# The opening and the end of a two-layer attention kernel: work moved between steps, the last batch in pairs of tiles, and products of zeros on TensorE

## Chip, cores and metric

One NeuronCore of a Trainium2 chip runs the whole program. The metric is the time of one execution on the device in microseconds: the median of the runs of the kernel before is 555.02 us (three runs, 554.78 to 560.3). A profiled execution of the same kernel took 555.56 us; the span that its trace covers is 553.7 us. "us" in all that follows is a time from the start of that span.

## What is computed

Four sequences (B = 4) of 512 tokens with 256 channels pass through two attention layers of 16 heads with 16 channels each. All inputs and outputs are 32-bit floats.

```
# layer 0
xn = x * rsqrt(mean(x*x) + 1e-6) * rms_w
scale, shift = split(cond @ w_cond)              # cond: (4, 512)
xm = xn * (1 + scale) + shift
q, k, v = split(xm @ w_qkv);  q, k = rope(q), rope(k)
x = softmax(q k^T / 4) v @ w_out + x
# layer 1
xn = layernorm(x, norm_w, norm_b)
q, k, v = xn @ q_w + q_b, xn @ k_w + k_b, (xn @ v_w + v_b) * mask
y = softmax(q k^T + (1 - mask) * -1e6) v
scale, shift = split(silu(cond) @ emb_w + emb_b)
h = layernorm(y, sb_norm_w, sb_norm_b) * (1 + scale) + shift
return x + silu(h) @ out_w + out_b
```

## The kernel before

**Tiles and groups.** Tokens lie in tiles of 128 partitions, `TPB` = 4 tiles a batch. The work on attention is cut into `GROUPS` = 32 groups: 2 layers x 4 batches x 4 groups of heads (`NG`), four heads in each. Group s is step s of one long loop, and a step has four parts, one for each tile k of 128 keys. For a head and a key tile, TensorE makes the scores of 128 keys against 512 queries (`score`, L393), adds the negative row maximum as a second product into the same PSUM bank (`shift`, L404), ScalarE takes the exponential (L561), and TensorE multiplies the probabilities by the values (`values`, L430) into one bank `ACC`. The row maxima come two steps earlier from products with queries and keys exchanged (`row_score`, L413), of which VectorE takes the maximum (L698 in layer 0, L695 in layer 1). Queries and keys are stored as two 16-bit parts each (q_parts, k_parts in device memory) and loaded back in another layout (q_s, k_s).

**Order.** Nothing is planned at run time: the order is written out by hand in tables, and each engine's function walks through the same loop `steps()` and picks its own instructions. `KEY_TILE` (L44) is the order inside one part of a step. `PIECES` (L83) says which other pieces come in which step and part: `turn` (transposes of normalised tokens, L465, with ScalarE's copy to xT, L586 or L599), `qk` (a projection of 128 query or key rows, L476), `v` (value projection, L487), `y` (output projection, L504), `modulate` and `embed` (two products with the condition vector, 32 small products each, L512). p0, f0, p1, f1 name the four places where tokens are turned: before the projections of layer 0, behind its attention, and the same for layer 1. `ROW_SCORES` says which row scores a part makes; steps 0 to 2 hold more than the others. Steps -3 to -1 are the opening, step 32 is the end. The same walk fixes the order of two rings of PSUM banks (`places`, L157): four banks for scores, turns and projections (ScalarE reads them), three for row scores, outputs, y, modulate and embed (VectorE reads them). A piece waits until the bank of its place is read. `turn_shift` (L438) turns the negated maxima, ScalarE copies them (L574) and SyncE moves them into the operand `shift` (L1091).

**Queues.** SyncE issues the loads of x, the tables and the later weights (L1100 to L1117), then `first_parts` (L1051 on) with the part stores of batch 0 (L1039), and the operand loads (L1074). VectorE's `opening` (L751 on) holds the statistics of x (L780 to L788), the normal tiles of batch 0 (L669), the modulation (L812) and the rotation of queries and keys of batch 0 (L798 to L805). ScalarE makes the high part of each (L664). POOL makes the powers (L966, L888), the normal tiles of the later batches, and the rotation of batches 1 to 3 (L912 to L920).

**End.** After the last values product ScalarE copies `ACC` (L568), TensorE turns it (L445), VectorE divides by the sums (L720, L722) and takes the statistics of all 256 channels (L728, L733), POOL makes the power (L886, L888), VectorE the normal tiles (L670), TensorE turns them (L465), ScalarE makes a linear and a tanh image (L599, L600), VectorE multiplies them (L849), TensorE makes the 16 output products (L504), VectorE adds the residual (L744), SyncE stores.

The parts of the two tables that matter:

```
-3: ((("modulate",),) + turn("p0", 0), qk(0, 0, 0, 1, 2, 3), v(0, 0)[:1] + turn("p0", 1) + v(0, 0)[1:],
     qk(0, 1, 0, 1, 2, 3) + v(0, 1)),
-2: (turn("p0", 2), qk(0, 2, 0), qk(0, 2, 1), qk(0, 2, 2)),
-1: (qk(0, 2, 3), (), (("embed",),), ()),
0: ((), (), *one(v(0, 2))),
```

## Time and profile before

| what | value |
|---|---|
| median of the runs | 555.02 us |
| the profiled execution | 555.56 us |
| its span | 553.7 us |
| mean granted TensorE clock over the span | 0.978 |
| busy in the span: TensorE | 516.7 us (93%) |
| VectorE | 408.5 us (74%) |
| ScalarE | 351.6 us (63%) |
| POOL | 213.1 us (38%) |
| moved by DMA | 45.23 MB, mean 82 GB/s |

Busy time is the time in which an engine has an instruction in flight; the products on TensorE are pipelined, so that their busy time says how long the engine has work and not how hard it works. The granted clock is given as a share of 2.4 GHz; 0.5 is 1.2 GHz. PEld is TensorE's weight load, which runs beside the products. A line of the timeline merges neighbouring instructions of the same kind: start, the time that the group takes together, engine, line, operation, output<-inputs, shape, count, and in brackets the idle time of the engine before it with what ended it.

### The profile page before, as it was taken

Reading aid. Unit: us, or ns where it says so; the run is one execution under the profiler, and the core shown is the slowest. Engines: PE = TensorE matmul, PEld = TensorE weight load, DVE = VectorE, ACT = ScalarE, POOL = GpSimd, SP = SyncE. Lnnn points to the kernel's source line nnn. Section 1 sums busy time; section 2 is a strip of 40 time slices with the busy share of each in tenths; the row PEclk is TensorE's granted clock in tenths of the full one; section 3 lists DMA queues with packets and bytes.
Section 4 is the critical chain, followed back from the end, with each engine's and each line's share of the span. In section 5 each row is a group of like instructions: output and inputs, shape, how many; then the busy total and the mean of one; then the engine's idle time right before and its main releaser. Section 6 shows DMA issues by size and latency. Waiting matters only on the chain. (4 is left out here: it accounts for less than half of the span.)

```text
span 553.7 us, 9732 instructions
## 1 busy us (share of the span) xinstructions
PE 516.7 (93%) x3296; PEld 197.1 (36%) x3296; DVE 408.5 (74%) x1056; ACT 351.6 (63%) x682; POOL 213.1 (38%) x223
## 2 busy tenths in 40 slices
PE   5788999999999999999999999999999999999945
PEld 5354432223333344234333344334234232423314
DVE  3586678778888667965898677966988998896032
ACT  1352346667757676776757675766786779678822
POOL 3139999249032350624242340624640034042200
PEclk9999898999999999999999999999999999999986
DMA  7963203143133133110421133111331211120001
GB/s 243 356 200 95 78 3 114 38 118 116 42 112 116 40 109 116 45 40 9 133 91 40 38 115 116 40 38 42 108 118 42 78 41 40 39 78 2 21 19 38
DMA packets 43016, 45.23 MB, mean 82 GB/s; under 512 B 4420, under 2 KB 41556, under 8 KB 42584
## 3 DMA queue, kind: packets, MB, share of 16 engines
q1 hardware_dynamic: 42680, 42.79, 24.7%
q10 hardware_dynamic: 288, 1.84, 0.9%
q8 instruction: 26, 0.43, 0.3%
q14 instruction: 22, 0.18, 0.1%
HBM read 25.46 MB, written 18.87 MB: 80 GB/s over the span
## 5 line engine op out<-in xcount | busy, mean ns | idle before, releaser
L561 ACT ACTIVATE probs<-bank 128x512 f32<-128x512 f32 x512 | 274.2, 597 | 102.7 <-PE bank L404 101.9
L413 PE MATMUL bank<-k_s,q_s 64*128 64x512 f16 x512 | 190.2, 388 | 8.8 <-DVE row_max L695 3.5
L698 DVE TENSOR_REDUCE row_max<-bank 128x1 f32<-128x512 f32 x256 | 162.1, 684 | 38.5 <-PE bank L413 37.0
L695 DVE CUSTOM_DVE_ANT_0 masked<-bank,mask_bias 128x512 bf16<-128x512 f32 x256 | 162.9, 687 | 19.7 <-PE bank L413 19.1
L393 PE MATMUL bank<-q_s,k_s 64*128 64x512 f16 x512 | 154.0, 384 | 1.1 <-ACT probs L561 0.6
L404 PE MATMUL bank<-shift,kx 64*128 64x512 f16 x512 | 150.3, 380 | 0.9 <-DMA shift<-shift_rows 0.9
L430 PE MATMUL bank<-probs,v_aug 128*17 128x512 f32 x1024 | 135.6, 601 | 0.7 <-ACT probs L561 0.7
L413 PEld LDWEIGHTS bank<-k_s,q_s 64*128 64x128 f16 x512 | 46.8, 93 | 167.4 <-DVE row_max L695 71.7
L476 PE MATMUL bank<-xT,wqkv 128*128 128x512 f32 x128 | 64.3, 634 | 5.2 <-ACT xT L586 5.2
L404 PEld LDWEIGHTS bank<-shift,kx 64*128 64x128 f16 x512 | 46.1, 95 | 29.7 <-DMA shift<-shift_rows 1.4
L898 POOL CAST parts<-plain 128x512 f16<-128x512 f32 x16 | 9.8, 611 | 72.6 <-ACT plain L612 72.6
L504 PE MATMUL bank<-wo,xT 128*128 128x256 f32 x128 | 33.7, 410 | 4.1 <-DVE xT L849 2.9
L393 PEld LDWEIGHTS bank<-q_s,k_s 64*128 64x128 f16 x512 | 31.1, 94 | 13.7 <-ACT probs L561 9.6
L476 PEld LDWEIGHTS bank<-xT,wqkv 128*128 128x128 f32 x128 | 23.1, 197 | 35.3 <-issue 31.4
L430 PEld LDWEIGHTS bank<-probs,v_aug 128*17 128x17 f32 x1024 | 17.0, 95 | 43.8 <-issue 23.7
L744 DVE TENSOR_TENSOR X<-bank,X 128x512 f32<-128x512 f32 x16 | 11.1, 692 | 27.7 <-PE bank L504 27.7
L487 PE MATMUL bank<-wqkv,xT 128*128 128x256 f32 x128 | 31.3, 389 | 0.0
L886 POOL TENSOR_SCALAR spread<-moments_f 128x4 f32<-128x4 f32 x4 | 0.9, 227 | 75.3 <-DVE moments_f L733 75.3
L504 PEld LDWEIGHTS bank<-wo,xT 128*128 128x128 f32 x128 | 24.6, 201 | 12.9 <-issue 6.7
L886 POOL TENSOR_SCALAR spread<-moments_p 128x4 f32<-128x4 f32 x4 | 0.9, 232 | 72.1 <-DVE moments_p L733 72.1
L720 DVE RECIPROCAL inv_sum<-bank 128x16 f32<-128x16 f32 x32 | 8.1, 252 | 26.5 <-PE bank L445 26.5
L487 PEld LDWEIGHTS bank<-wqkv,xT 128*128 128x128 f32 x128 | 23.2, 190 | 8.4 <-issue 5.6
(88 smaller groups left out, 491.9 us busy)
## 6 DMA issues: line engine op xcount, KB each, us to landing
q_parts<-parts SPq DMA_DIRECT2D x64, 128.0 KB
k_parts<-parts SPq DMA_DIRECT2D x64, 128.0 KB
q_s<-q_parts SPq DMA_DIRECT2D x32, 256.0 KB, 2.7
k_s<-k_parts SPq DMA_DIRECT2D x32, 256.0 KB, 3.0
X<-in_x SPq DMA_DIRECT2D x4, 512.0 KB, 7.3
y<-X SPq DMA_DIRECT2D x8, 256.0 KB, 2.7
wc<-in_w_cond ACTq DMA_DIRECT2D x1, 1024.0 KB, 5.0
tables<-in_tables SPq DMA_DIRECT2D x4, 256.0 KB, 7.0
```

Source lines behind the costliest of these rows:

```text
L393: nc.tensor.matmul(bank, m.k_s[slot][rows, i, keys], m.q_s[slot][rows, i, :], start=True, stop=False)
L404: nc.tensor.matmul(a_bank(m, A["score", s, k, h]), keys, m.shift[s % SHIFTS][rows, i, :], start=False, stop=True).then_inc(q.a_made, 1)
L413: nc.tensor.matmul(bank, m.q_s[slot][rows, i, queries], m.k_s[slot][rows, i, :], start=True, stop=True).then_inc(q.d_made, 1)
L430: last = nc.tensor.matmul(m.ACC[W32 * h:W32 * h + W, :], m.v_aug[pu % VALUES][:, k, G * g + h, :], m.probs[k][:, h, :], start=(k == 0), st ...
L476: last = nc.tensor.matmul(bank, m.wqkv[layer][:, k, i * P:(i + 1) * P], m.xT[use % 2][:, k, :], start=(k == 0), stop=(k == CT - 1))
L487: last = nc.tensor.matmul(bank[:, t * C:(t + 1) * C], m.xT[use % 2][:, k, at], m.wqkv[layer][:, k, 2 * C:3 * C], start=(k == 0), stop=(k = ...
L504: last = nc.tensor.matmul(bank[:, t * C:(t + 1) * C], m.xT[use % 2][:, k, at], m.wo[layer][:, k, :], start=(k == 0), stop=(k == CT - 1))
L561: act.activation(m.probs[k][:, h, :], bank, ACT.Exp, scale=1.0 if s >= B * NG else float(DH) ** -0.5)\
L695: dve.tensor_tensor_reduce(m.masked[D["max", n, k, h] % ND][:, :], bank, m.mask_bias[:, b, :], 1.0, LOWEST, ALU.add, ALU.max, to)\
L698: dve.tensor_reduce(to, bank, AX.X, ALU.max).then_inc(q.d_done, 1)
L744: dve.tensor_tensor(to, bank.rearrange("p (t c) -> p t c", c=C), to, ALU.add).then_inc(q.d_done, 1)
L898: pool.tensor_copy(m.parts[:, 0, i, :], m.plain[pu % 2][side][:, c, :]).then_inc(q.rope_pool, 1)
```

## The change

The change touches both ends of the loop and adds products of zeros.

- **Order before the first score.** Steps below 0 use `OPENING_TILE`: the row scores of heads 1, 3 and 0 stand ahead of the pieces, that of head 2 behind them. `PIECES` moves v(0,2) from step 0 to step -1 (in the place of the embedding), turn p0 3 from step 1 to step 0, and the four qk(0,3) each one to three parts up. The embedding is cut into four pieces (steps 1 to 3), with a VectorE instruction each; POOL's modulation of layer 1 stands behind its wait for the late data.
- **VectorE's opening** makes the modulation ahead of the statistics of batch 1. A new fill of a tile `idle` (128 x 512, 16-bit zeros) stands first.
- **SyncE** loads queries(0) behind all part stores of batch 0.
- **Products of zeros** (`keep_busy`), 128 x 128 by 128 x 512, into a bank that nobody reads: 11 ahead of the conditioning, 8 behind it, 6 behind the second half of the first turn, 14 behind the turns of the last output, 7 behind the turned tokens of the last batch.
- **The end.** The step behind the last group falls away; `last_batch` does the same work on the last batch by pairs of tiles: a copy for each pair, its turns, division, statistics of the last 64 channels (those of the first 192 are taken in step 31, `EARLY`), power, normal tiles. Then tanh by pair on ScalarE, the linear image and the product on VectorE by pair and half, four output products for each tile into a bank of its own, an addition for each tile, and three stores (two tiles, one, one) instead of two.

```diff
+OPENING_TILE = (("max", 1), ("max", 3), ("max", 0), ("pieces", None), ("turns", None), ("max", 2))
...
-    -1: (qk(0, 2, 3), (), (("embed",),), ()),
-    0: ((), (), *one(v(0, 2))),
-    1: ((), (), turn("p0", 3), qk(0, 3, 0)),
-    2: ((), qk(0, 3, 1), (), qk(0, 3, 2)),
-    3: (qk(0, 3, 3), (), (), ()),
+    -1: (qk(0, 2, 3), (), *one(v(0, 2))),
+    0: ((), (), turn("p0", 3), qk(0, 3, 0)),
+    1: ((), qk(0, 3, 1), (("embed", 0),), qk(0, 3, 2)),
+    2: ((), qk(0, 3, 3), (("embed", 1),), (("embed", 2),)),
+    3: ((("embed", 3),), (), (), ()),
     4: ((), *one(v(0, 3)), ()),
...
-PIECES[GROUPS] = ((), (), (), turn("f1", B - 1) + y(1, B - 1))
+LAST = B - 1
+PAIRS = TPB // 2
+EARLY = (NG - 1) * G * DH
+FIRST_BUSY = (11, 8, 6)
+LAST_BUSY = (14, 7)
...
 def steps():
-    for s in range(FIRST, GROUPS + 1):
+    for s in range(FIRST, GROUPS):
...
+    def keep_busy(count, bank):
+
+        for _ in range(count):
+            nc.tensor.matmul(bank, m.idle[:, 0:P], m.idle[:, :], start=True, stop=True)
+
+    def last_batch():
+        values(GROUPS - 1, KT - 1)
+        pe.wait_ge(q.d_done, len(D))
+        for p in range(PAIRS):
+            pe.wait_ge(q.last_copied, p + 1)
+            for t in pair(p):
+                last = nc.tensor.transpose(m.d_banks[p][:, t % 2 * P:(t % 2 + 1) * P], m.oT[:, t * P:(t + 1) * P],
+                                               m.ident[:, :])
+            last.then_inc(q.last_turned, 1)
+        keep_busy(LAST_BUSY[0], m.d_banks[2])
+        for p in range(PAIRS):
+            for t in pair(p):
+                pe.wait_ge(q.last_normal, t + 1)
+                for h in range(CT):
+                    last = nc.tensor.transpose(m.a_banks[CT * p + h][:, t % 2 * P:(t % 2 + 1) * P],
+                                               last_normal(m)[:, t, h * P:(h + 1) * P], m.ident[:, :])
+            last.then_inc(q.last_tokens, 1)
+        keep_busy(LAST_BUSY[1], m.d_banks[2])
+        for p in range(PAIRS):
+            pe.wait_ge(q.last_silu, CT * (p + 1))
+            for t in pair(p):
+                for k in range(CT):
+                    last = nc.tensor.matmul(sum_bank(m, t)[:, 0:C],
+                                            last_tokens(m)[:, k, t * P:(t + 1) * P], m.wo[1][:, k, :],
+                                            start=(k == 0), stop=(k == CT - 1))
+                last.then_inc(q.last_sum, 1)
+
+    pe.wait_ge(q.idle_made, 1)
+    keep_busy(FIRST_BUSY[0], m.a_banks[NA - 1])
...
+                if piece == ("turn", "p0", 0, 1):
+                    keep_busy(FIRST_BUSY[2], m.a_banks[NA - 1])
...
-                    conditioning(piece, m.condT)
+                    conditioning(piece, m.condT, range(KC))
+                    keep_busy(FIRST_BUSY[1], m.a_banks[NA - 1])
... (ScalarE)
+    def last_batch():
+        act.wait_ge(q.values_done, KT * GROUPS)
+        act.wait_ge(q.d_made, D["output", GROUPS - 2] + 1)
+        for p in range(PAIRS):
+            act.activation(m.oT[:, columns(p)], m.ACC[:, columns(p)], ACT.Copy).then_inc(q.last_copied, 1)
+        act.wait_ge(q.silu_made, CT * LAST)
+        for p in range(PAIRS):
+            act.wait_ge(q.last_tokens, p + 1)
+            for h in range(CT):
+                act.activation(m.tanh[h][:, columns(p)], m.a_banks[CT * p + h][:, 0:2 * P], ACT.Tanh,
+                               bias=m.mod1[:, 1, h, LAST:B], scale=m.mod1[:, 0, h, LAST:B]).then_inc(q.last_tanh, 1)
... (VectorE)
+        dve.memset(m.idle[:, :], 0.0).then_inc(q.idle_made, 1)
...
+        modulate()
         token_statistics(1, 1, 2)
-        modulate()
         token_statistics(2, 2, 3)
...
+    def last_batch():
+        O = m.O[LAST % 2]
+        steps_done = TPB
+        for p in range(PAIRS):
+            at = slice(2 * p, 2 * p + 2)
+            bank = m.d_banks[p][:, 0:2 * P].rearrange("p (t h w) -> p t h w", t=2, h=G)
+            dve.wait_ge(q.last_turned, p + 1)
...
+            for t in pair(p):
+                dve.bn_stats(m.last_stats[:, t, 1, :], O[:, t, EARLY:C]).then_inc(q.last_step, 1)
...
+            dve.tensor_scalar(m.last_spread[:, at], m.last_moments[:, at, 1], 1e-5, None, ALU.add)\
+               .then_inc(q.last_spread, 1)
+        dve.wait_ge(q.a_made, turned(NORMAL[-3]))
+        for t in range(TPB):
+            dve.wait_ge(q.last_rstd, t // 2 + 1)
+            dve.tensor_scalar(last_normal(m)[:, t, :], O[:, t, :], m.last_moments[:, t, 0:1], m.last_rstd[:, t:t + 1],
+                              ALU.subtract, ALU.mult).then_inc(q.last_normal, 1)
...
+        for p in range(PAIRS):
+            for h in range(CT):
+                dve.wait_ge(q.last_tanh, CT * p + h + 1)
+                dve.tensor_scalar(m.halved[h][:, columns(p)], m.a_banks[CT * p + h][:, 0:2 * P], m.mod1[:, 0, h, LAST:B],
+                                  m.mod1[:, 1, h, LAST:B], ALU.mult, ALU.add).then_inc(q.last_halved, 1)
+                dve.wait_ge(q.last_halved, CT * p + h + 1)
+                dve.scalar_tensor_tensor(last_tokens(m)[:, h, columns(p)], m.tanh[h][:, columns(p)], 1.0,
+                                         m.halved[h][:, columns(p)], ALU.add, ALU.mult).then_inc(q.last_silu, 1)
+        dve.wait_ge(q.bias_added, B)
+        for t in range(TPB):
+            to = m.X[:, TPB * LAST + t, :]
+            dve.wait_ge(q.last_sum, t + 1)
+            dve.tensor_tensor(to, sum_bank(m, t)[:, 0:C], to, ALU.add).then_inc(q.last_added, 1)
... (SyncE)
         for i in range(4):
-            if i == 3:
-                load_queries(0)
             for part, made in ((0, q.high_made), (1, q.part_dve)):
                 sp.wait_ge(made, i + 1)
                 send_part(sp, m, q, 0, i, part)
-        for i in range(4):
+        load_queries(0)
+        for i in (2, 3):
             sp.wait_ge(q.parts_out[i], chunk_out(0))
         load_keys(0)
```

## Rows read from the trace of the kernel before

**Rows 1.** Stretches: busy time of each engine, PEclk, DMA share, GB/s.

```profile
30.00:40.00 10.00, 8.20 (x26) 4.35 (x25) 9.08 (x22) 5.09 (x9) 3.98 (x5) 1.00 0.63 184
...
70.00:520.00 450.00, 440.29 (x2980) 153.89 (x2980) 357.33 (x933) 317.91 (x624) 172.42 (x173) 1.00 0.22 68
520.00:553.70 33.70, 20.39 (x112) 11.12 (x104) 8.59 (x22) 11.13 (x20) 1.26 (x2) 0.80 0.09 32
```

**Rows 2.** Timeline of the opening, until the first rotation product.

```profile
5.99 6.99 PE L512 MATMUL bank<-condT,wc 128*128 128x4 f32 x32 [5.99 <-DMA condT<-in_condT]
...
10.60 1.14 DVE L669 TENSOR_SCALAR XN<-X,rstd_p 128x256 f32<-128x256 f32 x4 [1.15 <-POOL rstd_p L966]
...
16.02 0.35 DVE L812 TENSOR_SCALAR mod_scale<-bank,vecs 128x4 f32<-128x4 f32 x2
...
18.21 9.60 PE L476 MATMUL bank<-xT,wqkv 128*128 128x512 f32 x16 [3.43 <-ACT xT L586]
18.88 1.41 DVE L780 BATCH_NORM_STATS2 stats<-X 128x6 f32<-128x256 f32 x4 [2.44 <-DMA X<-in_x]
...
25.11 0.69 DVE L798 TENSOR_TENSOR roped<-plain,tables 128x512 f32<-128x512 f32 x1 [4.02 <-ACT plain L615]
```

**Rows 3.** Groups by form, TensorE, 18.1 to 23.2: busy, mean ns.

```profile
L476 PE MATMUL bank<-xT,wqkv 128*128 128x512 f32 x6 | 5.3, 1058 | 3.4 <-ACT xT L586 3.4
```

**Rows 4.** Timeline, from the first part store to the first score and behind it.

```profile
27.82 5.76 SPq L1039 DMA_DIRECT2D q_parts<-parts  x8
...
37.74 2.47 SPq L1039 DMA_DIRECT2D k_parts<-parts  x4
...
40.88 3.62 PE L487 MATMUL bank<-wqkv,xT 128*128 128x256 f32 x16
...
44.85 0.39 PE L413 MATMUL bank<-k_s,q_s 64*128 64x512 f16 x1 [0.36 <-DMA k_s<-k_parts]
...
47.69 1.98 PE L476 MATMUL bank<-xT,wqkv 128*128 128x512 f32 x4
...
51.09 1.98 PE L476 MATMUL bank<-xT,wqkv 128*128 128x512 f32 x4
...
59.44 3.73 PE L512 MATMUL bank<-es,wc 128*128 128x4 f32 x32
...
63.10 0.39 PE L393 MATMUL bank<-q_s,k_s 64*128 64x512 f16 x2
...
63.96 8.46 DVE L698 TENSOR_REDUCE row_max<-bank 128x1 f32<-128x512 f32 x14
...
64.74 3.64 POOL L669 TENSOR_SCALAR XN<-X,rstd_p 128x256 f32<-128x256 f32 x4
```

**Rows 5.** Timeline of the end, behind the last values product.

```profile
532.84 0.60 ACT L568 ACTIVATE oT<-bank 128x512 f32<-128x512 f32 x1 [1.17 <-PE bank L430]
...
539.82 1.94 PE L465 MATMUL bank<-ident,XN 128*128 128x128 f32 x8 [5.61 <-DVE XN L670]
...
544.65 5.78 PE L504 MATMUL bank<-wo,xT 128*128 128x256 f32 x16 [2.89 <-DVE xT L849]
...
550.47 0.69 DVE L744 TENSOR_TENSOR X<-bank,X 128x512 f32<-128x512 f32 x1 [1.34 <-PE bank L504]
```

**Rows 6.** Stretches again: one behind the first score, two of the end.

```profile
65.00:66.00 1.00, 1.00 (x7) 0.35 (x3) 1.00 (x3) 0.22 (x1) 1.00 (x2) 0.50 0.68 205
...
535.00:541.00 6.00, 1.18 (x6) 1.21 (x7) 3.17 (x12) 0.01 (x1) 1.26 (x2) 0.52 0.00 0
...
548.00:553.70 5.70, 2.43 (x9) 1.71 (x8) 1.38 (x2) 0.00 (x0) 0.00 (x0) 0.92 0.27 92
```

**Rows 7.** Timeline: eight transposes and eight output products at the full clock.

```profile
45.17 1.09 PE L465 MATMUL bank<-ident,XN 128*128 128x128 f32 x8
...
521.10 1.99 PE L504 MATMUL bank<-wo,xT 128*128 128x256 f32 x8
```

**Rows 8.** Groups by form from 532 us on: busy, mean ns.

```profile
L888 POOL TENSOR_TENSOR rstd_f<-spread,minus_half 128x4 f32<-128x4 f32 x1 | 1.0, 1037 | 0.1
```

More of the change, by code:

```diff
@@ L200, in await_read, with pair, columns, last_normal @@
         engine.wait_ge(q.d_made, D["y", layer, b, 1] + 1)
+def pair(p):
+    return range(2 * p, 2 * p + 2)
+def columns(p):
+    return slice(2 * p * P, (2 * p + 2) * P)
+def last_normal(m):
+    return m.XN[(len(NORMAL) - 1) % 2]
+def sum_bank(m, t):
+    return m.d_banks[t] if t < ND else m.ACC
+def last_tokens(m):
+    return m.xT[(len(USES) - 1) % 2]
 class Buffers:
@@ L506, in tokens_out, with conditioning @@
         last.then_inc(q.d_made, 1)
-    def conditioning(piece, vector):
+    def conditioning(piece, vector, chunks):
         bank = d_free(D[piece])
-        for c in range(KC):
+        for c in chunks:
             for k in range(KC):
@@ L845, in vector @@
                 if piece[0] == "embed":
-                    embed()
-                if piece[0] == "turn" and piece[1:3] == ("f1", B - 1):
-                    i, h = silu_ready(dve, q, piece)
-                    dve.scalar_tensor_tensor(m.xT[i][:, h, :], m.tanh[h], 1.0, m.halved[h], ALU.add, ALU.mult)\
-                       .then_inc(q.silu_made, 1)
+                    embed(piece)
         for n, j in row_scores(s, k):
@@ L853, in vector @@
                 negate(n)
+    last_batch()
 def silu_ready(engine, q, piece):
```

126 lines of the change are left out of this document (86 added, 40 removed).

## Prediction

> **What bounds the kernel now.** I read the table of stretches first [rows 1]: from 70 to 520 us TensorE is busy for 440.3 of 450 us and VectorE, the next, for 357.3; from 520 on TensorE is idle for 13.3 of 33.7. The middle is a full TensorE queue. What starts that queue earlier comes off the span one for one, and so does what shortens the tail behind the last attention product.
>
> In the timeline of the opening [rows 2] the reader is to see a chain and not a full engine: conditioning products until 13.0; VectorE's modulation at 16.0, behind its statistics of batch 1; projections from 18.2; the first rotation product on VectorE at 25.1, after 4.02 us idle. Further on [rows 4] the stores leave from 27.8, the first row score is at 44.85, the first score at 63.1. At the end [rows 5] each step waits for all of the one before it: copy, turn, divide, statistics, power, normalise, turn, silu, 16 products, add, store.
>
> The clock is the second thing. Before its first recorded change the clock column reads 1.00, but durations say 1.2 GHz: six projection products take 5.3 us [rows 3], later four take 1.98; 32 conditioning products take 6.99 us [rows 2] and 3.73 for the embedding [rows 4]. At the end the granted clock is 0.52 from 535 to 541 us [rows 6]; there eight transposes take 1.94 us and 16 output products 5.78 [rows 5]. At 2.4 GHz eight transposes take 1.09 and eight output products 1.99 [rows 7], a pitch of 0.13 and 0.23.
>
> **The opening up to the first row score.** Eleven zero products start behind a new VectorE fill, at about 1.4 us. No row shows a 16-bit product of 128 rows by 512 columns. Below it lies the 64-row one (a single one 0.39 with its latency, some 0.2 in a row), above it the 32-bit projection (0.43 a product at 2.4 GHz); it has the type and the columns of the first, so I take 0.21, and 0.43 at 1.2 GHz. Eleven at 0.43 are 4.7 us and end at 6.1; the conditioning could start at 5.99. Cost 0.1. Conditioning then takes between 3.7 and 7.0 us, by the clock: until 9.8 or 13.1. Eight zero products take 1.7 or 3.4, eight transposes 1.1 or 1.9, six more zero products 1.3 or 2.6 (ScalarE makes its two xT tiles beside these). VectorE's modulation moves ahead of the statistics of batch 1: with its normal tiles done at 11.7 it comes at 11.8 to 13.9 instead of 16.0. With the high clock throughout, the projections would start at 14.2; with a low clock for the conditioning and a rise in the eight, at about 16.5. Either beats 18.2, and they then run at 0.43 apiece. Two chunks (eight products, 3.4 us) and a copy (0.6) have VectorE's operand ready at 18.3 to 20.6.
>
> VectorE does not start then: its statistics of batch 2 wait for a DMA until 18.88, and it is idle from 21.1 (25.11 less 4.02) [rows 2], an order that the change keeps. So the rotation starts at 21.15 instead of 25.11: **−3.95**. That DMA is what is late next. From there a chain of VectorE and ScalarE that the change leaves alone leads on. SyncE issues 16 part stores, eight in 5.76 us [rows 4], so 11.5 in all, from 23.9: until 35.4, plus the landing. The load of queries(0) moves behind the last store: the last four left at 37.74 behind that load, they go some 0.6 earlier, and the queries' 0.5 us of issue now stand just ahead of the keys'. The DMA engines' share of 0.63 from 30 to 40 us [rows 1] is 6.3 us of work, which 6 us less time would just hold: between 0 and 2 us of the gain may be lost there. I take none, as the loss begins only when the share passes 1. TensorE's own queue before the first row score ends at 44.5 (40.88 and 3.62) [rows 4], so at 40.6 then, and caps any larger gain. First row score near 40.9.
>
> **Row scores to the first score.** The order max 1, 3, 0, pieces, 2 replaces max 1, pieces, 3, 0, 2. From product to VectorE it is 0.43, a maximum 0.62, a projection chunk 1.92. With three banks, max 0 waits for max 2 of the tile before: 0.43 + 0.62 + 0.1 + 0.22 + 1.92 = 3.3 us a tile against 3.4 (51.09 less 47.69) [rows 4]. Over four tiles, the first with a turn only, the last maximum comes 1.2 us earlier; but the shift row is turned behind a projection and copied behind that projection's copy, so 0.3 to 0.65 remains. Two value pieces (16 products of 256 columns, 3.6 us) take the place of the embedding (3.73) as TensorE's cover while the shift row is stored and lands, some 3 us: **−0.65** at the first score. Without that cover TensorE would wait for those 3 us.
>
> **Pieces moved between steps.** v(0,2) leaves step 0 (two pieces of 1.99), turn p0 3 comes to step 0 from step 1, the four qk(0,3) move up by one to three tiles, and the embedding comes back as four pieces of 0.93. After the first score that is −3.98 + 3.73 = **−0.2**. VectorE's embedding work (0.6) no longer stands ahead of its first maxima there: **−0.2**. POOL's normal p0 3 ends at 68.4 now [rows 4], at 64.4 then; its turn, in the third tile of step 0 (10 us behind the first score), is due near 68.5: covered by 4 us. The modulation of layer 1 moves behind POOL's late-data wait, long before its first use in step 22: nothing. The clock was low in a stretch around 65 us [rows 6], but VectorE ran 14 maxima through it without a pause [rows 4], so TensorE waited for it: its absence is priced 0, with 1 us as the bound.
>
> **The end.** The last products of values stop at 532.8. From there by pair, with durations of full-size rows [rows 5, 8]: the copy of 256 columns lies between half of 0.60 and 0.60, taken 0.38 (a fixed part of 0.17 does not shrink); two transposes, on VectorE at 533.75. Reciprocal 0.25, multiply 0.29, two statistics of 64 columns 0.37 (the other 192 are done a step earlier, in VectorE's idle time), two aggregations 0.26, an add 0.16: 1.35 a pair, so 535.1 and 536.45. The power costs 1.04 for four columns, and I take as much for two: 536.2 and 537.5. Normal tiles (0.35) end at 537.2 and 538.3, since VectorE does pair 1's statistics ahead of pair 0's normals. Turned: 537.6 and 538.65. The tanh of 256 columns (taken 0.5; a copy of 512 takes 0.60) runs four times, until 539.7, beside VectorE. VectorE's halved (0.43) and product (0.42, between half of 0.69 and 0.69), four times, are the chain: from 538.3 to 540.1 for pair 0, 541.8 for pair 1. Sums at 0.9 a tile: 541.1, 542.0, 542.9, 543.9. Last add 544.4. From the last add's end to the span's end it is 2.54 (551.16 to 553.7), kept. End 546.9: **−6.8**. The 14 and the 7 zero products end at 537.1 and 540.15, as their successors' operands come, if the clock is high.
>
> Between the two bursts only transposes run. They take 1.94 us for eight at 0.5 and 1.09 at 1.0 [rows 5, 6, 7]; no row shows whether they hold a clock. If they don't, that is rival B. The Trainium skill, page "TensorE: Matmul & The Clock Gate", Part 4, says that transposes do not count as TensorE being busy; by it the clock could fall there, and the sum would be 547.0.
>
> **Sum.** 3.95 + 0.65 + 0.2 + 0.2 + 6.8 = 11.8 less: the profiled execution goes from a span of 553.7 to 541.9, and from 555.56 to 543.8. The median of the runs shown stands 0.54 under the profiled one: **543.3**. Bounds: 2 lost to DMA, 1 gained in the low stretch, 1.5 either way for half-size durations: 540 to 547.
>
> **Rivals.**
> A. Zeros do not raise the clock, and each product stands in the queue at 0.43. Opening: 6.1, 13.1, 16.5, transposes 18.5, six more 21.1 against 18.2: +2.9. End: 540.1 after the 14, 542.1, 545.1 after the 7, 550.9 after 16 sums in 5.8, add and store 553.9: +0.2. With the −1.05 of the moves: 557.0, slower than before, inside 1%. It decides where the projections start after 18.2. For it: nothing here shows what a product of zeros does. Against it: dense products brought the clock up before 28 us and after 548 [rows 6], whatever their values. 6%.
> B. The clock is low for the 7 products and the 16 sums: +1.5 and +2.2. For it: the clock is low from 535 [rows 6], behind the turns that follow the copy of 532.84 [rows 5], and TensorE stays as empty as now until 534. 547.0. 17%.
> C. The opening's gain goes to the DMA queue or another wait before the first score, 3 to 4 us: 546.8. 12%.
> D. Low stretches before 90 us go too and VectorE's last chain is shorter: 540. 12%.
> E. An embedding piece in the ring of three banks, with the maxima queued behind it, or a late turn p0 3 stalls steps 0 to 3 for 5 us: 549.5 with a little of C. 4%.
>
> **How the numbers follow.** The forecast has 49%. Its 540 to 547, B and C to 548.5, D from 539.5: about 80% in 539.5 to 548.5. A measurement of this kernel tells about 1% (5.55 us) from no change: faster needs under 549.5, which the forecast, D and nearly all of B and C give: 0.88; same 0.10 (A, E, tails); slower, over 560.6: 0.02.
>
> **What would show it.** First rotation product at 21.2 (above 23: the clock or a preload decided); first row score near 41; first score near 58.6; last values at 528, which is 532.8 less 5.0; from them to the span's end 14.1 against 20.9; granted clock 1.00 through the last 14 us. The sum is wrong if the first score comes early and the last values do not, or if zero products run at 0.43 near the end.

## The result and the profile after

The changed kernel takes 543.81 us (median of four executions, 543.0 to 545.67), beside 557.53 us for the kernel before (four executions, 554.78 to 560.3): a ratio of 0.9743, 95% interval 0.9695 to 0.9791. Forecast were 543.3 us and a range of 539.5 to 548.5. Four more executions later gave 544.08 to 547.67; all eight together have a median of 544.86.

The profiled execution is the slowest of its four: 545.67 us, span 543.8, against 555.56 and 553.7. Its stretches come first (columns as in [rows 1]).

```profile
9.90:13.00 3.10, 3.10 (x8) 1.14 (x7) 1.47 (x7) 0.00 (x0) 0.69 (x1) 0.50 1.03 367
...
30.00:40.00 10.00, 9.82 (x22) 4.92 (x23) 7.87 (x18) 3.54 (x7) 7.58 (x9) 0.83 0.87 271
70.00:520.00 450.00, 440.66 (x3007) 155.93 (x3001) 356.19 (x935) 318.14 (x625) 168.38 (x169) 1.00 0.22 68
520.00:543.80 23.80, 19.36 (x113) 9.10 (x109) 12.12 (x38) 7.94 (x16) 1.52 (x2) 1.00 0.13 45
...
536.00:543.80 7.80, 4.93 (x22) 3.17 (x19) 4.57 (x11) 0.66 (x2) 0.00 (x0) 1.00 0.20 67
```

TensorE's busy time in the middle is that of before, 440.66 against 440.29 us [rows 1], so the time was saved at the two ends. The granted clock is 1.00 through the end, where it was 0.52 from 535 to 541 us [rows 6].

The timeline of the opening (start, us, engine, line, operation; some zeros now stand in it) answers to [rows 2] and [rows 4]:

```profile
1.18 4.87 PE L575 MATMUL bank<-idle 128*128 128x512 f16 x11 [1.18 <-DVE idle L859]
...
5.98 3.86 PE L568 MATMUL bank<-condT,wc 128*128 128x4 f32 x32
...
9.70 3.49 PE L575 MATMUL bank<-idle 128*128 128x512 f16 x8
...
11.69 0.34 DVE L920 TENSOR_SCALAR mod_scale<-bank,vecs 128x4 f32<-128x4 f32 x2
...
15.30 7.11 PE L532 MATMUL bank<-xT,wqkv 128*128 128x512 f32 x16
...
19.23 1.41 DVE L888 BATCH_NORM_STATS2 stats<-X 128x6 f32<-128x256 f32 x4 [2.87 <-DMA X<-in_x]
...
21.36 0.69 DVE L906 TENSOR_TENSOR roped<-plain,tables 128x512 f32<-128x512 f32 x1
...
24.07 5.76 SPq L1194 DMA_DIRECT2D q_parts<-parts  x8
```

The projections start at 15.30 instead of 18.21, the rotation at 21.36 instead of 25.11, straight behind the statistics of batch 2. These wait for the load of x until 19.23 and not for TensorE. The stores leave 3.75 earlier than at 27.82.

Further on, TensorE's projections before the first row score, the row score itself, and what lies around the two small instructions that negate the maxima:

```profile
30.18 8.73 PE L532 MATMUL bank<-xT,wqkv 128*128 128x512 f32 x16 [3.44 <-ACT xT L680]
38.75 3.62 PE L543 MATMUL bank<-wqkv,xT 128*128 128x256 f32 x16
42.30 0.60 PE L469 MATMUL bank<-k_s,q_s 64*128 64x512 f16 x3
...
55.15 1.26 POOL L1061 TENSOR_TENSOR roped<-plain,tables 128x512 f32<-128x512 f32 x1 [0.17 <-ACT plain L709]
...
55.45 0.99 DVE L813 TENSOR_SCALAR neg_max<-row_max 128x16 f16<-128x16 f32 x1
56.38 1.26 POOL L1062 TENSOR_TENSOR roped<-plain,tables 128x512 f32<-128x512 f32 x1
56.48 1.19 DVE L815 SCALAR_TENSOR_TENSOR neg_max<-row_max,neg_max 128x16 f16<-128x16 f32 x1
...
57.81 0.22 PE L494 MATMUL bank<-ident,neg_max 128*32 128x128 f16 x1 [1.21 <-DVE neg_max L815]
...
61.61 0.39 PE L449 MATMUL bank<-q_s,k_s 64*128 64x512 f16 x2
...
81.18 0.39 PE L460 MATMUL bank<-shift,kx 64*128 64x512 f16 x2 [0.93 <-DMA shift<-shift_rows]
```

The key operand lands before TensorE wants it; the first row score at 42.30 starts when TensorE's own queue is through. It was at 44.85, so 2.55 of the opening's 3.75 are left; the first score comes at 61.61 against 63.10 and keeps 1.49. The negations of 128 x 16 numbers take 0.99 and 1.19 us, each until the POOL product beside it ends (56.41 and 57.64), and TensorE's turn of the shift row (L494) waits 1.21 us for the second.

The timeline of the end answers to [rows 5]:

```profile
529.69 0.66 ACT L732 ACTIVATE oT<-bank 128x256 f32<-128x256 f32 x2 [1.17 <-PE bank L486]
...
530.68 3.19 PE L575 MATMUL bank<-idle 128*128 128x512 f16 x14
...
532.18 0.73 POOL L1178 TENSOR_TENSOR last_rstd<-last_spread,minus_half 128x2 f32<-128x2 f32 x1 [18.99 <-DVE last_spread L954]
...
533.53 0.80 POOL L1178 TENSOR_TENSOR last_rstd<-last_spread,minus_half 128x2 f32<-128x2 f32 x1 [0.63 <-DVE last_spread L954]
...
535.40 0.54 DVE L967 TENSOR_SCALAR tables<-bank,mod 128x256 f32<-128x256 f32 x1 [0.29 <-ACT tables L737]
535.43 1.67 PE L575 MATMUL bank<-idle 128*128 128x512 f16 x7
...
537.37 3.82 PE L599 MATMUL bank<-wo,xT 128*128 128x256 f32 x16 [0.26 <-DVE xT L970]
...
541.23 0.42 DVE L976 TENSOR_TENSOR X<-bank,X 128x256 f32<-128x256 f32 x1 [0.44 <-PE bank L599]
```

From the copy at 529.69 to the span's end it is 14.11 us, before 20.86 (532.84 to 553.7). The 16 output products take 3.82 instead of 5.78 us.

### The profile page after: what moved, and what is told of

It reads as the page before. It is cut to its first block, busy times and chain, and to the rows that moved or that the text cites. A ratio compares the mean times of both kernels' runs of the same rounds, so it can differ in the third digit from the quotient of the medians.

```text
span 543.8 us, 9837 instructions
## 1 busy us (share of the span) xinstructions
PE 521.1 (96%) x3342; PEld 195.9 (36%) x3342; DVE 413.6 (76%) x1073; ACT 350.6 (64%) x683; POOL 213.3 (39%) x223
## 4 chain that ended last, share of the span: by engine, by line
PE 71%; DVE 19%; issue 3%; DMA 3%; ACT 1%; SPq 1%; DVEq 0%; ACTq 0%
PE bank L486 17%; PE bank L469 11%; PE bank L532 10%; PE bank L460 8%; PE bank L449 8%; DVE masked L802 7%; PE bank L560 5%; PE bank L543 5%; DVE row_max L805 5%; DMA X<-in_x 3%; PE bank L521 2%; PE bank L501 2%; DVE stats L835 2%; DVE X L851 1%; ACT probs L655 1%
## 5 line engine op out<-in xcount | busy, mean ns | idle before, releaser
L469 PEld LDWEIGHTS bank<-k_s,q_s 64*128 64x128 f16 x512 | 46.9, 93 | 164.4 <-DVE row_max L802 71.1
L560 PE MATMUL bank<-wo,xT 128*128 128x256 f32 x112 | 27.9, 392 | 1.2 <-DVE row_max L805 0.6
L851 DVE TENSOR_TENSOR X<-bank,X 128x512 f32<-128x512 f32 x14 | 9.7, 692 | 22.5 <-PE bank L560 22.5
L709 ACT ACTIVATE plain<-bank 128x512 f32<-128x512 f32 x16 | 9.5, 595 | 22.5 <-PE bank L532 22.5
L560 PEld LDWEIGHTS bank<-wo,xT 128*128 128x128 f32 x112 | 20.1, 189 | 8.6 <-issue 3.4
```

Of the source, the lines that this page charges most:

```text
L469: nc.tensor.matmul(bank, m.q_s[slot][rows, i, queries], m.k_s[slot][rows, i, :], start=True, stop=True).then_inc(q.d_made, 1)
L560: last = nc.tensor.matmul(bank[:, t * C:(t + 1) * C], m.xT[use % 2][:, k, at], m.wo[layer][:, k, :], start=(k == 0), stop=(k == CT - 1))
L851: dve.tensor_tensor(to, bank.rearrange("p (t c) -> p t c", c=C), to, ALU.add).then_inc(q.d_done, 1)
```

## The experiments

All times are medians in us; the ratio is to the kernel before on the same chip, with its 95% interval. The runs stand in three sets: e1, e2, e4 and e5 beside 559.56 us of the kernel before, c1, e3, e6 and e7 beside 558.71, e8 to e11 beside 559.25.

| run | what it is | us (lowest to highest, executions) | ratio |
|---|---|---|---|
| e1_no_zeros_first | no zeros in the opening | 545.57 (545.22–547.32, 4) | 0.9767 [0.9726, 0.9808] |
| e2_no_zeros_last | no zeros at the end | 547.52 (546.81–548.09, 4) | 0.9796 [0.9749, 0.9842] |
| e3_no_zeros | neither | 547.82 (546.64–549.12, 4) | 0.9815 [0.9763, 0.9867] |
| c1_again | the changed kernel again | 545.86 (544.08–547.67, 4) | 0.9778 [0.9713, 0.9843] |
| e4_fill | 16 more zeros before the second projections | 545.32 (544.66–545.73, 4) | 0.9755 [0.9716, 0.9794] |
| e5_pool_wait | POOL waits ahead of a rotation | 544.30 (543.38–545.37, 4) | 0.9738 [0.9698, 0.9779] |
| e6_fill_pool_wait | e4, and the wait inside an earlier rotation | 544.96 (544.26–545.39, 4) | 0.9762 [0.9713, 0.9812] |
| e7_end_only | opening of before, changed end | 552.64 (547.86–553.31, 4) | 0.9883 [0.9818, 0.9947] |
| e8_old_pieces | old tables of pieces and row scores | 547.78 (544.69–550.95, 4) | 0.9814 [0.9756, 0.9873] |
| e9_old_modulate | modulation behind the statistics of batch 1 | 544.95 (544.40–546.71, 4) | 0.9769 [0.9718, 0.9819] |
| e10_turn1_early | shift row of group 1 turned one part earlier | 544.24 (543.05–545.23, 6) | 0.9749 [0.9708, 0.9791] |
| e11_combined | e10, the wait of e6, 11 zeros only in the opening | 546.07 (544.93–547.51, 6) | 0.9787 [0.9742, 0.9832] |

Times of one kernel spread by up to 4 us (the kernel before 7.6), so much of what follows is read from profiles: the start of the rotation, the first row score, the first score, the first and the last copy of `ACC`, and the span.

| profile | rotation | row score | first score | first copy | last copy | span |
|---|---|---|---|---|---|---|
| before | 25.11 | 44.85 | 63.10 | 88.01 | 532.84 | 553.7 |
| changed | 21.36 | 42.30 | 61.61 | 85.20 | 529.69 | 543.8 |
| changed again (c1) | 23.08 | 42.39 | 60.72 | 85.61 | 530.16 | 544.3 |
| e1 | 22.65 | 42.53 | 60.58 | 84.91 | 529.83 | 544.0 |
| e2 | 21.89 | 41.19 | 59.51 | 84.40 | 528.86 | 545.5 |
| e3 | 21.82 | 41.13 | 59.46 | 83.22 | 528.14 | 544.8 |
| e4 | 21.64 | 40.95 | 59.27 | 85.27 | 529.81 | 543.9 |
| e5 | 20.89 | 40.20 | 58.52 | 82.94 | 527.46 | 541.6 |
| e6 | 21.79 | 41.90 | 59.95 | 84.51 | 529.11 | 543.2 |
| e7 | 25.07 | 45.56 | 66.64 | 92.19 | 536.25 | 550.4 |
| e8 | 21.73 | 41.05 | 59.59 | 84.42 | 528.77 | 542.9 |
| e9 | 22.69 | 42.01 | 60.33 | 84.64 | 529.21 | 543.3 |
| e10 | 22.04 | 43.04 | 62.32 | 84.67 | 529.22 | 543.3 |
| e11 | 22.08 | 41.51 | 59.56 | 84.00 | 528.91 | 543.0 |

### What the zeros are worth

```diff
-FIRST_BUSY = (11, 8, 6)
+FIRST_BUSY = (0, 0, 0)        # e1_no_zeros_first, e3_no_zeros
-LAST_BUSY = (14, 7)
+LAST_BUSY = (0, 0)            # e2_no_zeros_last, e3_no_zeros
```

> The changed kernel without its 25 products of zeros in the opening (11, 8, 6); those of the end stay. Theory: they are what puts the conditioning (3.86 us in the changed kernel, 6.99 before) and the first projections at the full clock. Without them the conditioning takes 7.0 us again and ends near 13, the first eight projections run at 0.85 apiece, and the first rotation product on VectorE comes near 23.5 instead of 21.36; the median is 1.5 to 2.5 us above the changed kernel's, near 545.5 to 546. Rival: the opening hangs on the DMA of batch 2 (VectorE's statistics at 19.23) and the modulation's new place, and the zeros are worth nothing: the rotation still starts at 21.4 and the median stays within 1 us of the changed kernel's 543.8.

> The changed kernel without its 21 products of zeros at the end (14, 7); those of the opening stay. Theory: the pairs alone bring most of the 6.7 us of the end, and the zeros only keep the clock: without them it falls to 0.5 some us behind the last values product, the 16 output products take 5.8 us instead of 3.8 and the last 8 transposes some 0.1 us more apiece; from the copy of ACC to the span's end 16.5 us instead of 14.1, against 20.9 before. Median 1.5 to 2.5 us above the changed kernel's. Rival: the clock stays at 1.00 without them, since there is now no idle time as long as before; then 14.1 and no difference.

> The changed kernel without any product of zeros. Theory: the two effects seen apart add up (about 1 us in the opening: first rotation at 22.65 instead of 21.4 without its zeros; 2.5 us at the end: 16.6 instead of 14.1 from the copy of ACC to the span's end), so 3 to 4 us above the changed kernel, 547.5 to 548.5; the order and the pairs alone keep about 7 to 8 of the gain over the kernel before. Rival: the zeros of the two ends stand in for one another or are all that is gained; then it is within 1 us of the changed kernel or within 1% of the kernel before.

> The changed kernel once more, as the one to compare the others of this set with. Its first profile was the slowest of its four runs (545.67 against 543.0 to 543.9) and showed the clock low from 30.1 to 33.6 us. Theory: whether that stretch occurs differs from one execution to the next; without it the first row score is near 40.5, the first score near 59, the span near 542. Rival: it is always there, and the first row score is again near 42.3.

**The end.** Stretches of e2, and its output products:

```profile
529.00:535.00 6.00, 2.62 (x12) 1.77 (x12) 3.97 (x19) 1.29 (x4) 1.53 (x2) 0.69 0.00 0
535.00:541.00 6.00, 4.23 (x11) 3.27 (x11) 4.25 (x10) 1.19 (x3) 0.00 (x0) 0.50 0.00 0
```

```profile
536.90 6.00 PE L599 MATMUL bank<-wo,xT 128*128 128x256 f32 x16 [1.77 <-DVE xT L970]
```

Without zeros the granted clock is 0.50 from 535 to 541, and the 16 products take 6.00 us instead of 3.82. From the last copy to the end it is 16.64 us (545.5 less 528.86) instead of 14.11; in e3 16.66. In the profiles of the changed kernel, c1, e1 and e7 it is 14.11 to 14.17. So of the end's 6.75 us the zeros give 2.5, and 4.2 are left for the work by pairs, which was not run with the old end beside it. Medians fit this: e2 lies 2.7 above the changed kernel's 544.86, e3 2.3 above e1 and 2.0 above c1 of its own set.

**The opening.** Here the zeros are worth 0.7 us by the medians (545.57 against 544.86), less than the spread; against c1 alone (545.86) they are worth nothing. The changed kernel's second profile shows why it is so little. TensorE alone:

```profile
1.17 4.87 PE L575 MATMUL bank<-idle 128*128 128x512 f16 x11 [1.17 <-DVE idle L859]
5.84 6.87 PE L568 MATMUL bank<-condT,wc 128*128 128x4 f32 x32
12.57 3.57 PE L575 MATMUL bank<-idle 128*128 128x512 f16 x8
15.93 1.61 PE L521 MATMUL bank<-ident,XN 128*128 128x128 f32 x8
17.38 1.46 PE L575 MATMUL bank<-idle 128*128 128x512 f16 x6
18.67 3.67 PE L532 MATMUL bank<-xT,wqkv 128*128 128x512 f32 x8
```

The same 11 zeros stand in front, but the conditioning took 6.87 us here and 3.86 in the first profile: by these durations the clock had risen in one execution and not in the other. The eight zeros then stand in the queue for 3.57 us, and the projections start at 18.67; without any zeros (e1) they start at 15.66, behind the same slow conditioning. That is rival A's mechanism, and here it decides the rotation: 23.08, behind a wait of 2.13 us for ScalarE's copy. In the eight profiles with all 25 zeros and the modulation at its new place the projections start between 15.30 and 18.67, without zeros at 15.66 (e1) and 15.69 (e3); but all 16 then take 7.03 to 7.11 us with zeros, and 9.68 and 8.58 without. So the zeros win 0.4 us of TensorE's start or lose up to 3.0, and give back some 1.5 to 2.6 in the projections. Mostly neither counts: in seven of the eight, and in e3, the rotation follows VectorE's statistics of batch 2 without a wait for ScalarE, at 20.89 to 22.04; c1 and e1 (22.65, after 1.14 us) wait for TensorE's chain.

### Where the first row score and the first score lose time

```diff
+                if piece == ("v", 0, 0, 1):
+                    keep_busy(16, m.d_banks[2])        # e4_fill, e6_fill_pool_wait
...
         for i in range(4):
+            if (b, i) == (1, 3):
+                pool.wait_ge(q.shift_made, 1)          # e5_pool_wait
             rope(b, i)
...
+        if (b, i) == (1, 2):
+            pool.wait_ge(q.shift_made, 1)              # e6_fill_pool_wait, e11_combined
         pool.tensor_tensor(m.parts[:, 1, i, :], x[:, :], m.parts[:, 0, i, :], ALU.subtract)
```

> The changed kernel with 16 more products of zeros, where TensorE waits 3.44 us for ScalarE's xT ahead of the second batch's projections (26.7 to 30.2 us). Theory: in the profiled execution of the changed kernel the clock fell at that wait, the next projections took 8.73 us instead of 7.11, and TensorE, which reached the first row score at 42.3 instead of 40.7, is what holds the opening up. With the clock kept the first row score comes at 40.7 and the span is 1.6 us shorter than the profiled 543.8 (the median gains less, 0 to 1.6, as the fall need not happen in every execution). Rival: the first row score is held by the load of the keys, issued at 36.97, or the gain is lost to the next wait before the first score at 61.6: then the first score stays there.

> The changed kernel with one more wait: POOL starts the last of batch 1's four rotations only when VectorE has made the first negated row maxima. Theory: these two small VectorE instructions took 0.99 and 1.19 us at 55.45 and 56.48 instead of 0.17 and 0.18, because POOL's two-input products run at that time and hold the SBUF port that both share. With POOL kept quiet they take 0.17 and 0.18 and the first score comes 1.5 to 1.9 us earlier (near 59.9 on the time base of the profiled execution of the changed kernel), the median up to 1.7 us lower. Rival: the long durations come from something else (VectorE's own wait for its last maximum, TensorE's bank); then they stay near 1 us and the first score stays at 61.6. Bound: POOL itself comes 1 us later, and its tile for the turn of batch 3 has some 7 us to spare.

> 16 more products of zeros ahead of the second batch's projections, and POOL's last product of batch 1's third rotation starts only when VectorE has made the first negated maxima. In the runs with the fill or with the wait at the fourth rotation the first negated maximum took 0.17 us and its low part 1.01, with POOL's last product of the third rotation running at that time (the wait stood behind it). Theory of the shared port: now both take under 0.2, and from the first row score to the first score it is 17.5 us instead of 18.3. Rival: the second one takes 1.01 whatever POOL does. For the whole time: the clock's low stretches near 65 us decide more than this; between 0 and 1 us lower than the fill alone.

**The fill.** With zeros in TensorE's pause before 30 us (e4) the 16 projections take 7.11 us instead of 8.73, and the first row score comes at 40.95 and the first score at 59.27. But the first copy of `ACC` is at 85.27, as without the fill. Its stretches of steps 0 and 1:

```profile
66.00:71.00 5.00, 5.00 (x22) 0.94 (x18) 3.63 (x7) 1.27 (x3) 4.76 (x6) 0.50 0.00 0
83.00:85.00 2.00, 2.00 (x9) 0.15 (x8) 1.50 (x3) 0.44 (x1) 1.92 (x2) 0.50 0.85 255
```

The clock is 0.50 in both, and TensorE busy throughout. In e3, whose first score is at 59.46 and whose clock is 1.00 throughout from there on, the first copy is at 83.22, 2.05 us earlier. So in this profile the gain was given back in low stretches, and the median, 545.32, shows none of it. The fill is not free either: from the first rotation to the first row score it is 19.30 to 19.32 us in seven profiles (c1, e2, e3, e4, e5, e8, e9), but 20.11 in e6, where the 16 zeros were still running when the tokens were ready, and the projections started 0.87 us later behind the rotation than in e4.

**The negation.** e5 held POOL at the wrong place: its negations took 0.17 and 1.01, as they do without a wait in c1, e2, e3, e4 and e9. e6 held it ahead of the product that collides. In e6's timeline the two negations of group 0, the turn of the shift row behind them, and then what became of those of group 1, on VectorE, POOL and TensorE:

```profile
55.06 0.17 DVE L815 TENSOR_SCALAR neg_max<-row_max 128x16 f16<-128x16 f32 x1
55.27 0.17 DVE L817 SCALAR_TENSOR_TENSOR neg_max<-row_max,neg_max 128x16 f16<-128x16 f32 x1
56.14 0.23 PE L494 MATMUL bank<-ident,neg_max 128*32 128x128 f16 x1
...
70.58 2.78 DVE L815 TENSOR_SCALAR neg_max<-row_max 128x16 f16<-128x16 f32 x1
```

```profile
69.72 1.15 POOL L1139 TENSOR_TENSOR mask_part<-mask_row,mask_part 4x512 f16<-4x512 f32 x1
...
70.84 1.26 POOL L1063 TENSOR_TENSOR roped<-plain,tables 128x512 f32<-128x512 f32 x1
72.07 1.26 POOL L1064 TENSOR_TENSOR roped<-plain,tables 128x512 f32<-128x512 f32 x1
...
74.23 0.39 PE L469 MATMUL bank<-k_s,q_s 64*128 64x512 f16 x1 [1.60 <-DVE row_max L807]
```

With POOL held, both take 0.17 us. From row score to first score it is 18.05 us in e6 and e11, where no negation is long; 18.32 in the six profiles in which one takes 1.01 or 1.02; and 19.31 and 19.28 in the changed kernel's first profile and in e10, where both are long. TensorE's turn of the shift row waits 1.21 and 1.17 us for the negation in those two, 0.21 or 0.22 in the six, and not at all in e6 and e11. In e1 the first negation takes 0.65 us and the second 0.17; TensorE does not wait, and it is 18.05 as well. So both together cost 1.26 us, one alone 0.27, and some half a microsecond is hidden behind TensorE's queue: that the negation is what the first profile lost there is shown.

Group 1 collides too. In e6 its negation takes 2.78 us, until the second POOL product ends at 73.33, and TensorE waits for 1.60; it had begun while a POOL product was running (until 70.87), and two more went ahead of it. But this is not the POOL wait's doing alone: without it the same negation took 1.99 us in c1 and e2, 2.02 in e3 and 1.65 in e8, with 0.81 to 0.84 of waiting on TensorE in the first three, and 0.47 to 0.94 in the changed kernel's first profile and in e1, e4, e5, e9 and e10. The two profiles with the wait of e6 have the longest, 2.78 and 2.76 (e6, e11). That the wait makes it longer is likely and rests on these two; the median of e6 is 544.96.

### What each part of the opening is worth

```diff
-    -1: (qk(0, 2, 3), (), *one(v(0, 2))),              # e7_end_only, e8_old_pieces
+    -1: (qk(0, 2, 3), (), tuple(("embed", c) for c in range(KC)), ()),
...                                                     # steps 0 to 3 as before
-    return KEY_TILE if s >= 0 else OPENING_TILE
+    return KEY_TILE                                    # e7_end_only, e8_old_pieces
...
-        modulate()
         token_statistics(1, 1, 2)
+        modulate()                                     # e7_end_only, e9_old_modulate
...
-FIRST_BUSY = (11, 8, 6)
+FIRST_BUSY = (0, 0, 0)                                 # e7_end_only
...
+            if i == 3:
+                load_queries(0)                        # e7_end_only
...
-        load_queries(0)
```

> The opening of the kernel before (order, modulation, SyncE's queue, no zeros there) with the end of the changed kernel, zeros included. The embedding is made in four pieces at its old place. Theory: ends and opening are independent, and the end is worth 6.7 us (copy of ACC to the span's end 14.1 instead of 20.9), so this lies 6 to 7.5 us under the kernel before and some 4 to 6 above the changed one. Rival: the last values product comes later for it (something of the end was hidden), or the opening is worth as little as the 3.15 us that the two first profiles show at the last values product.

> The changed kernel with the pieces and the order inside the steps below 0 of the kernel before (embedding, in four parts, where v(0,2) stands now); modulation, SyncE's queue and zeros as changed. Theory: the first row score is as early as in the changed kernel (40.2 to 42.4), as the modulation's place and the DMA of batch 2 set it, but from there to the first score it is 19 to 21 us instead of 18.3 (embedding of 3.7 to 5.0 us, four reads on VectorE ahead of its first maxima) and step 0 holds two value pieces: 1 to 3 us above the changed kernel at the last values product. Rival: the new order is worth nothing, since TensorE has the same work; then the last values product is within 0.5 us of the changed kernel's.

> The changed kernel with one thing undone: VectorE makes the modulation behind the statistics of batch 1, as before. Theory: it comes at 16.1 instead of 11.7, ScalarE's xT tiles at 16.6, the projections at 18.2 with the full clock, so two chunks and a copy make VectorE's operand ready at 22.3: the first rotation comes near 22.3 instead of 21.4 to 21.9, about 0.5 to 1 us later in the median. Rival: with the clock at 1.00 the first rotation does not depend on it and the DMA of batch 2 alone decides; no difference.

With the opening of before and the changed end (e7) it is 552.64, some 6 below the kernel before of that set (558.71) and 7.8 above the changed kernel's 544.86. The end is worth what its spans say (6.75); the opening is worth more than its 3.15 in the first pair of profiles: 7.8 by this, 6.8 against c1 of the same set (545.86). One of e7's four executions took 547.86. e7's profile shows the surplus, in its timeline and its stretches:

```profile
59.46 0.73 DVE L813 TENSOR_SCALAR neg_max<-row_max 128x16 f16<-128x16 f32 x1
60.23 1.19 DVE L815 SCALAR_TENSOR_TENSOR neg_max<-row_max,neg_max 128x16 f16<-128x16 f32 x1
...
61.71 5.00 PE L568 MATMUL bank<-es,wc 128*128 128x4 f32 x32
```

```profile
64.00:77.00 13.00, 13.00 (x51) 4.99 (x51) 8.91 (x16) 4.34 (x8) 12.54 (x13) 0.50 0.30 82
```

Its row score is at 45.56, 0.7 later than in the profile of before, but its first score at 66.64, 3.5 later: here the negations took 0.73 and 1.19 us where the profile of before has 0.17 and 0.18 (58.76 and 58.97), the embedding 5.00 where [rows 4] have 3.73, and the clock was low for 13 us. The order of before meets both hazards too, and in its profiled execution, at the fast end of its runs, it happened to miss them. Whether its slower executions, up to 561.4 us, are those that meet them is not shown: none of them was profiled.

e8, with old pieces and order under all other changes, has 547.78 and a spread from 544.69 to 550.95; by its interval it can't be told from the changed kernel. In its profile, which is its fastest execution, it is 18.54 us from row score to first score, where 19 to 21 were expected, and the last copy is no later than in the changed kernel's two; so what the new order is worth stays open. In e9 the old place of the modulation puts the rotation at 22.69, after 1.06 us of waiting for ScalarE, and the median does not show it. Read with e1 and e3 this says that the zeros and the modulation's place stand in for one another: the rotation is at 22.69 with the zeros alone, at 22.65 and 21.82 with the new place alone, at 20.89 to 23.08 with both, and at 25.07 and 25.11 with neither (e7, before).

### Two attempts at a better version

```diff
-TURN_AT = {0: (-1, 1), 1: (0, 3), 2: (1, 2), 3: (2, 2)}
+TURN_AT = {0: (-1, 1), 1: (0, 2), 2: (1, 2), 3: (2, 2)}   # e10_turn1_early, e11_combined
-FIRST_BUSY = (11, 8, 6)
+FIRST_BUSY = (11, 0, 0)                                   # e11_combined, with the POOL wait of e6
```

> The changed kernel with the turn of group 1's shift row one part earlier (third part of step 0 instead of the fourth). In all runs so far TensorE waits 0.9 us for that row at the start of step 1 (its store is issued 2.5 us before), and step 1's first part takes 5.4 us, or 6.5 where the clock is low at that point. Theory: the wait goes, and the low stretch that followed it in three runs goes with it: the first part of step 1 takes 4.5 to 4.8, 0.7 to 1 us less in all, up to 2 where the clock stays up. Rival: VectorE, which has eight maxima in that part (4.84 us), is what sets it; then it only waits elsewhere and the gain is under 0.3 us.

> All that the runs so far point to: the turn of group 1's shift row one part earlier; POOL's last product of batch 1's third rotation behind the first negated maxima; and of the opening's zeros only the first 11. Theory: the 8 and the 6 stand in the queue ahead of the turned tokens, and cost 3.4 and 2.6 us where the clock has not risen by then (first rotation at 23.1 in the repeat), while the DMA of batch 2 hides what they bring where it has; without them the first rotation comes at 21.4 to 22.0 in every run. 1 to 2 us under the changed kernel's median. Rival: without the 8 and the 6 the projections run at the low clock and the first rotation comes at 22.7 as without all zeros; then the gain is that of the turn alone.

In the changed kernel TensorE waits 0.93 us at 81.18 for the shift row of group 1 (the profile after, above). In e10 that wait is gone:

```profile
80.28 0.60 PE L449 MATMUL bank<-q_s,k_s 64*128 64x512 f16 x2
80.50 0.59 PE L460 MATMUL bank<-shift,kx 64*128 64x512 f16 x2
```

From the first score to the first copy it takes 22.35 us instead of 23.59, but this execution negated its maxima in 0.96 and 1.19 us and had its first score at 62.32. Its median of 544.24 is 0.6 below the changed kernel's 544.86, which the spread doesn't tell from nothing. In e11 the chain of waits runs through the long negation of group 1:

```profile
65.89 4.28 DVE row_max L805 x7
...
70.19 2.77 DVE neg_max L813
...
72.98 0.19 DVE neg_max L815
...
73.30 0.22 PE bank L494
```

An earlier turn needs the negation of group 1 earlier. With the earlier turn alone (e10) it took 0.68 us; in e11, with POOL's wait too, 2.76. That the two edits work against each other is likely, not shown: e11 also leaves out 14 zeros, and such a negation was long without the wait in other profiles. Its median is 546.07. No version here is shown to beat the changed kernel.

## Why the prediction was right, point by point

**The end: right, with errors that cancelled.** 14.1 us was forecast and 14.11 measured. The power took 0.73 and 0.80 for two columns where I took 1.04, half of the linear image 0.54 where I took 0.43, four times on VectorE's chain; so the sums ended 0.4 later behind the copy than forecast (11.50 against 11.06), and the tail from the last addition to the span's end was 0.4 shorter (2.15 against 2.54). That the total meets the forecast to 0.01 is luck; that each step is within half a microsecond is not. Rival B did not come about: between the zeros the clock stayed at 1.00 across transposes, eight in two times 0.76. In e2, without zeros, it was low for the 16 sums, as in B, and cost 2.5, less than the 3.7 that I priced.

**The opening: the rotation right, by the step given.** 21.15 forecast, 21.36 measured, set by the statistics that wait for DMA and not by TensorE. In the other profiles with the same zeros and modulation it is 20.89 to 22.04, again behind these statistics, and 23.08 in c1, where TensorE's start decides. Rival C's queue of transfers did not limit in this profile: 0.87 DMA share from 30 to 40 us, and the keys were ready before TensorE. In e1 TensorE waited 0.50 us for the keys.

**The first row score: late by 1.4.** 40.9 forecast, 42.30 measured. I priced the 16 projections of batch 1 at the high clock; behind a pause of 3.44 us they ran into a low stretch (30.1 to 33.5) and took 8.73 instead of 7.11. e4 filled the pause and had 40.95. Unfilled pauses of 1.79 to 2.31 us kept the clock in c1, e1, e2, e3, e5, e8, e9 and e11 (7.10 or 7.11), and one of 2.30 in e10 did not (8.80). Where the clock holds, the row score comes 19.3 us behind the rotation, at 40.20 to 41.19 for a rotation at 20.89 to 21.89: the forecast chain is right for those executions.

**The step that failed: "Row scores to the first score", −0.65.** It measured +1.06 in the profiled execution (19.31 against 18.25). The negations, which the profile of before shows at 0.17 and 0.18, were carried over at that size; they stretch over POOL's products when they meet them, and moving VectorE's work against POOL's moved them into one. In six profiles of this order one negation takes 1.01 or 1.02, and it is 18.32; e6 shows the term with none: 18.05, so −0.2 rather than −0.65 even then. The sum had taken the upper end of its own 0.3 to 0.65. The tile period stayed at 3.4 (projections at 48.98 and 52.39) and did not fall to 3.3, and the last maximum came 0.8 us earlier instead of 1.2: from the row score to the first negation it is 13.15 where it was 13.91.

**Behind the first score: better than priced.** −0.4 forecast; first score to first copy went from 24.91 to 23.59, −1.32. The low clock was not free, as I had it: the first part of step 1 takes 5.4 us where the clock is high (after, e3, e6) and 6.5 where it is low (before, c1, e2, e4, e8). The profile of before has two low stretches there, 64.2 to 71.0 and 84.7 to 88.1, that of after one, 67.7 to 71.1.

**The sum.** The last values moved by −3.15 and not −5.0 in the profiled execution, and the span by −9.9 and not −11.8. The missed 1.85 of the last values is +1.4 up to the first row score, +1.7 up to the first score, −0.9 up to the first copy and −0.3 in the middle (444.83 us between first and last copy before, 444.49 after). The slow projections and the second long negation are not in every profile, and the other three executions have spans of 541.2 to 542.1, about the sum's 541.9; that they lack these two is likely and not shown, as they were not profiled. That the median met the forecast within 0.5 us is in part luck: the profiled execution lies 1.9 above its forecast of 543.8, and the same kernel had 545.86 in the repeat, 2.6 above 543.3. The ratio came out a little better than forecast because the kernel before, 555.02 in three runs, had 557.53 with a fourth and 558.71 to 559.56 in later sets.

## What to carry to other kernels

Products of zeros pay where TensorE would otherwise idle through a serial tail right before dense work (2.5 us here, for nothing on the path); ahead of work that may already be ready they stand in the queue and win little. A short VectorE instruction on the critical path must be priced with what POOL runs beside it, and a wait on POOL that frees one such instruction must be checked against the next. Where single profiles of both kernels differ by such coincidences, undo one part at a time and compare several profiles before an opening is called faster or slower.

## What the runs showed of the hardware

- **Two small VectorE instructions did not end before POOL's product beside them.** A VectorE instruction on 128 x 16 numbers took 0.17 us alone, and 0.99, 1.19 and 2.78 beside POOL's two-input products of 1.26; each time it ended within 0.05 us of the end of a POOL product, and the longest spans the rest of one product and two whole ones. The Trainium skill, page "SBUF — State Buffer", section "Who interferes with whom", says that the two engines share a pair of ports as an exclusive lock, taken by a VectorE instruction in a two-port mode or with two inputs in SBUF, and held by whoever issues first until it ends. The traces agree for both instructions; but in e6 POOL's next two products went ahead of a VectorE instruction that was already waiting. That POOL is held up in the same way no run here shows.
- **Zeros count as work for the clock, and transposes between them did not lose it.** In the last 14 us the granted clock was 1.00 with the zeros and 0.50 without (535 to 541 in e2). The transposes ran between 14 zeros and seven more; transposes alone were not tried.
- **The first rise of the clock is not the same in each execution.** Behind the same 11 zeros the conditioning took 3.86 us once and 6.87 once; in the eight other runs that have them it took 4.01 to 5.08.
- **The clock fell during or right behind rows of small products.** In the profile after it is 0.50 from 9.9 to 13.0 (first stretch shown), behind 32 conditioning products of four columns in which TensorE had no pause (5.98 to 9.70); the eight zeros there took 3.49 us, where 14 took 3.19 at the end. Of the ten profiles with zeros ahead of the conditioning, all but c1 show this fall, between 8.2 and 10.2 us. In e7 it is 0.50 from 64 us, inside the 32 products of the embedding (61.71 to 66.64), after 1.93 us idle. Whether the small products or a pause before them caused it no run here separates.
